# A post-layernorm transformer block on one core: the order of the last group's residuals and roots, and ScalarE's f16 high halves of the first two groups' rows eight steps earlier

## What is computed

```
x = layernorm(x + attention(x))     # 16 heads of 16, l2-normalised q and k, window of 128, alibi bias
x = layernorm(x + ffn(x))           # 256 -> 1024 -> 256
def ffn(x):
    h = gelu(x @ bw1.T + b1)        # bw = mean(|w|, axis=1) * sign(w)
    return h @ bw2.T + b2
```

## Time and profile before

| what | value |
|---|---|
| median of 3 runs | 369.43 us |
| the profiled execution | 370.22 us |
| its span, first to last instruction | 368.4 us |
| TensorE busy | 353.2 us (96%) |
| VectorE busy | 308.7 us (84%) |
| ScalarE busy | 307.3 us (83%) |
| GpSimd busy | 285.4 us (77%) |
| granted TensorE clock, mean | 0.997 |

### The profile page before, as it was taken

The page is one execution under the profiler, slowest core; times in us unless marked ns, Lnnn a source line. Parts: engine busy times, 40 slices in busy tenths (PEclk is TensorE's granted clock), DMA queues, the critical chain, the costliest instruction groups (busy, mean ns, idle before and its releaser), DMA issues. The chain is left out here.

```text
span 368.4 us, 13096 instructions
## 1 busy us (share of the span) xinstructions
PE 353.2 (96%) x4461; PEld 244.1 (66%) x4461; DVE 308.7 (84%) x771; ACT 307.3 (83%) x532; POOL 285.4 (77%) x440
## 2 busy tenths in 40 slices
PE   8789999999999999999999999999999999999992
PEld 5555676667766776776677677675666667667682
DVE  5977899898898898898899988879777887786775
ACT  3588888898898998898899999988888888887753
POOL 1188999889989999998999999757756856856433
PEclk9999999999999999999999999999999999999998
DMA  7678944744655646667767773303303513413113
GB/s 231 143 117 186 185 109 98 157 99 94 137 120 106 142 96 132 139 159 154 156 144 155 153 147 74 59 4 59 59 0 59 115 45 72 114 39 76 59 59 114
DMA packets 106884, 40.19 MB, mean 109 GB/s; under 512 B 92128, under 2 KB 105824, under 8 KB 106720
## 3 DMA queue, kind: packets, MB, share of 16 engines
q1 hardware_dynamic: 106848, 39.73, 49.6%
HBM read 12.72 MB, written 4.19 MB: 46 GB/s over the span
## 5 line engine op out<-in xcount | busy, mean ns | idle before, releaser
L1341 POOL TENSOR_SCALAR_AFFINE_SELECT prob<-prob 128x512 f32<-128x512 f32 x252 | 153.7, 646 | 11.1 <-ACT prob L700 11.1
L700 ACT ACTIVATE prob<-ps 128x1024 f32<-128x1024 f32 (+1 forms) x128 | 122.2, 1009 | 13.5 <-PE ps L390 13.4
L551 PE MATMUL ps<-yT,sgn 128*128 128x512 f16 x256 | 61.1, 379 | 0.0
L772 ACT ACTIVATE ps<-ps,bias,alpha 128x512 f32<-128x512 f32 x64 | 47.9, 750 | 15.6 <-PE ps L551 12.5
L421 PE MATMUL ps<-wqkv,xt 128*128 128x512 f32 x124 | 58.7, 596 | 1.2 <-DVE qkn L952 1.1
L411 PE MATMUL ps<-prob,vdiag 128*17 128x128 f32 x1024 | 51.3, 274 | 0.3
L411 PE MATMUL ps<-prob,vnext 128*17 128x128 f32 x992 | 49.9, 273 | 0.0
L1409 POOL TENSOR_TENSOR resid<-z,resid 128x256 f32 (+1 forms) x31 | 22.5, 726 | 29.9 <-DVE z L1173 29.9
L551 PEld LDWEIGHTS ps<-yT,sgn 128*128 128x128 f16 x256 | 25.0, 98 | 22.6
L390 PE MATMUL ps<-qkT 64*64 64x192 f16 (+2 forms) x1024 | 33.7, 248 | 2.8 <-DMA qkT<-parts 2.7
L454 PE MATMUL ps<-wo,oT 128*128 128x256 f32 x128 | 36.2, 405 | 0.1
(11 more groups left out here) (113 smaller groups left out, 690.2 us busy)
## 6 DMA issues: line engine op xcount, KB each, us to landing
xt<-in_xT SPq DMA_DIRECT2D x32, 128.0 KB, 2.1
resid<-in_x SPq DMA_DIRECT2D x32, 128.0 KB, 2.2
out_dram<-resid SPq DMA_DIRECT2D x7, 512.0 KB, 2.9
w<-in_w2T SPq DMA_DIRECT2D x1, 1024.0 KB, 7.7
w<-in_w1T SPq DMA_DIRECT2D x4, 256.0 KB, 3.3
w_nat<-in_w SPq DMA_DIRECT2D x4, 256.0 KB, 3.3
wqkv<-in_wqkvT SPq DMA_DIRECT2D x3, 256.0 KB, 3.9
qkT<-parts SPq DMA_TRANSPOSE x39, 4.3
```

The source lines that it names most:

```text
L551: mm = nc.tensor.matmul(ps[:, bank, :], sgn1[:, c, P * k:P * k + P], yT[:, par, a, c, :, :], start=(m == 0), stop=(m == 2 * DC - 1))
L700: nc.scalar.activation(to, scored, ACT.Exp, scale=QK_SCALE ** -2).then_inc(exp_done, 1)
L772: nc.scalar.activation(bank, bank, ACT.Gelu, bias=bias1[:, k:k + 1], scale=alpha1[:, k:k + 1]).then_inc(gelu_done, 1)
L1341: return nc.gpsimd.affine_select(out=at, in_=at, compare_op=ALU.is_ge, fill=0.0, base=-near, pattern=[[0, CH], [1 if near else -1, P]], ch ...
```

## The change

Two edits that don't touch each other.

The first: on ScalarE the loop now covers steps 4 to 15, and steps 16 to 23 are written out with one `high_y` at the end of each: group 0 in steps 16 to 19, group 1 in steps 20 to 23. They are gone from steps 24 to 29, and `high_pair` is gone.

The second, in the last group. VectorE takes both statistics of rows 0 and 1 ahead of `scale_out(g, 2)`, goes through the first half of the last block, and only then makes the shift for group 6; the shift for rows 0 and 1 comes after the last block's aggregate; rows 2 and 3 wait for roots 2 and 3 each by itself. GpSimd adds the residuals of rows 0 and 1 ahead of group 6's root, and the roots of group 7 are now of three columns (rows 0 to 2) and of one (row 3), in place of two and two.

```diff
-            with act.Fori(0, (NB - 12) // XS) as t:
+            with act.Fori(0, (NB - 20) // XS) as t:
                 for n in range(XS):
                     step(t * XS + 4 + n, n)
+            for n in range(2):
+                for b in range(XS):
+                    step(NB - 16 + n * XS + b, b, tail=lambda n=n, b=b: high_y(n, b, n))
...
-            step(NB - 8, 0, amid=lambda: signs1(0), tail=lambda: high_y(0, 0, 0))
+            step(NB - 8, 0, amid=lambda: signs1(0))
...
-            step(NB - 3, 1, next3=False, before_rows=lambda: signs2(1), tail=lambda: high_y(1, 1, 1))
+            step(NB - 3, 1, next3=False, before_rows=lambda: signs2(1))
...
             take_strips(NB - 2)
-            high_pair()
             gelu_of(0, 3, 0)
...
                 scale_out(g, 0, LAST_ZBANKS)
                 scale_out(g, 1, LAST_ZBANKS)
+                statistics(g, 0, 1)
+                statistics(g, 1, 1)
+                scale_out(g, 2, LAST_ZBANKS)
+                last_half(0)
                 end_shift(0, zmv[:, 0, :, 0], sixth)
-                statistics(g, 0, 1)
-                scale_out(g, 2, LAST_ZBANKS)
-                statistics(g, 1, 1)
-                last_half(0)
                 dve.wait_ge(zlast_sum, 1)
                 statistics(g, 2, 1, NB)
-                end_shift(1, zmv[:, 1, 0:2, 0], first)
                 last_half(1)
...
                 nc.vector.bn_aggr(zmv[:, 1, GB - 1, :], last_stats[:]).then_inc(zaggr, 1)
-                dve.wait_ge(end_rooted, 3)
+                end_shift(1, zmv[:, 1, 0:2, 0], first)
                 for b in (2, 3):
                     m = NB - GB + b
+                    dve.wait_ge(end_rooted, b)
...
                 pool.wait_ge(zaggr, summed)
+                count(pool, end_rooted, n)
...
+            add_residual(NG - 1, 0)
+            add_residual(NG - 1, 1)
             end_root_of(0, NB - GB, zmv[:, 0, :, 1], slice(0, GB))
-            for b in range(GB - 1):
-                add_residual(NG - 1, b)
-            end_root_of(1, NB - 2, zmv[:, 1, 0:2, 1], slice(GB, GB + 2))
-            end_root_of(2, NB, zmv[:, 1, 2:4, 1], slice(GB + 2, 2 * GB))
+            add_residual(NG - 1, 2)
+            end_root_of(1, NB - 1, zmv[:, 1, 0:3, 1], slice(GB, GB + 3))
+            end_root_of(2, NB, zmv[:, 1, 3:4, 1], slice(GB + 3, 2 * GB))
```

More of the change, by code:

```diff
@@ L741, in signs1, with high_y @@
                 nc.scalar.activation(sgn1[:, :, cols], w1_t[:, :, cols], ACT.Sign).then_inc(sgn_ready, 1)
+            def high_y(n, b, par):
+                act.wait_ge(y_done, n * GB + b + 1)
+                count(act, y_in[par], (n - par) * 8)
+                nc.scalar.activation(yparts[:, par, 0, :, b, :], resid4[:, n * GB + b, :, :], ACT.Copy).then_inc(yhi_done, 1)
             nc.scalar.preload_act_table_set("natural_log_exp_and_others")
@@ L796, in activate @@
                         high_y(n + 1, 3, 1 - par)
-            def high_pair():
-                high_y(1, 2, 1)
-                high_y(1, 3, 1)
             def last_signs():
@@ L806, in last_signs @@
                 signs2(3)
-            step(NB - 8, 0, amid=lambda: signs1(0), tail=lambda: high_y(0, 0, 0))
[L809 to L812, removed]
-            step(NB - 3, 1, next3=False, before_rows=lambda: signs2(1), tail=lambda: high_y(1, 1, 1))
+            step(NB - 8, 0, amid=lambda: signs1(0))
+            step(NB - 7, 1, amid=lambda: signs1(1))
+            step(NB - 6, 2, amid=lambda: signs1(2))
+            step(NB - 5, 3, amid=lambda: signs1(3))
+            step(NB - 4, 0, amid=lambda: signs2(0))
+            step(NB - 3, 1, next3=False, before_rows=lambda: signs2(1))
             step(NB - 2, 2, next2=False, next3=False, before_rows=last_signs)
```

## The result

The changed kernel takes 372.37 us (median of 6 runs, 371.75 to 372.69) against 369.55 us for the kernel before in the same comparison: a ratio of 1.0063, 95% interval [1.0033, 1.0093], or 2.3 us slower with 1.2 to 3.4 as bounds. A second comparison, of the same file, gave 1.0059 [1.0040, 1.0078]. The ratio is estimated apart from the medians and need not be their quotient, which is 1.0076 in the first comparison; so the loss is 2.3 us by the ratio and 2.8 by the medians. The forecast had the sign and both places. Its size, +1.2 us, was about half of what came, and the time lies above its range of 369.0 to 371.5.

The account below looks back on a forecast made before the run. With TensorE busy 353.2 of 368.4 us, only its mid-kernel gaps and the end after its last matmul could bring time. Terms 0 + 0 + 0.9 + 0.3 = +1.2 us gave a median of 370.6, range 369.0 to 371.5.

Parts of the forecast that it names:

- High halves in steps 16 to 23: Attention steps 16 to 23: ScalarE's idle time hides eight added operations; 0, kept between -0.1 and +0.4 us.
- High halves out of steps 24 to 29: Attention steps 24 to 29: ScalarE loses six operations, but GpSimd and VectorE set the pace; 0, ends -0.8 and +0.3 us.
- Rival (c): Steps 24 to 29 lose their gaps: -0.8, with +1.2 elsewhere 369.8 us; chance 0.10.
- high_pair: Before `outputs`: GpSimd's bias additions start early and hold four VectorE operations, so TensorE waits for `otok`; +0.9 us, bounds 0 to 1.4.
- 0.24 + 0.36 + 0.47 = about 1.1: Waits of VectorE's first and third small operations and of L961 beside GpSimd's additions, about 1.1 us together.
- The second slips in: VectorE's second small operation before `outputs` runs right behind the first without waiting for a GpSimd addition.
- The 0.36 for the third: Wait of VectorE's third small operation before `outputs`, taken as L870's: 0.53 - 0.16 us.
- The rule of the Trainium skill: VectorE's second SBUF port is shared with GpSimd and the two block each other, so the early additions cost time.
- The end: After 357.80 us: group 6's store goes out later and three stores queue at 345 GB/s; +0.3 us, from +0.1 to +0.35.
- rival (b): Last stores overlap better than one queue at 345 GB/s; end gains 0.5 to 0.7, time 368.8 to 369.0 us; chance 0.10.
- Rival (d): Steps 16 to 23 pay as VectorE comes late: +0.4 or more, 371.0 to 371.5 us; chance 0.60 together with the forecast.

Follow-up runs that it names:

- the gated kernel: High halves early, end as before, and GpSimd's eight bias additions made to wait until VectorE has made otok of block NB - 2: level with the kernel before.
- The parts: Two kernels, each with one edit against the kernel before: high halves alone, medians 1.5 us apart; end alone, medians 0.75 us apart.
- the third order: Kernel before with group 6's shift inside the last block's first half, ratio 1.0005; second form, rows 0 and 1's shift ahead of the second half, 0.9979.

## Why the prediction was right and wrong

**High halves in steps 16 to 23: right.** Forecast 0. ScalarE is busy 1.3 us more there, TensorE's eight steps take 57.31 in place of 57.44, and the gated kernel is level with before. The windows of exactly these steps, after and then before:

```profile
127.93:185.24 57.31, 57.31 (x912) 40.34 (x913) 51.86 (x128) 52.14 (x96) 52.99 (x81) 1.00 0.66 140
```

```profile
128.70:186.14 57.44, 57.44 (x913) 40.33 (x913) 51.61 (x128) 50.86 (x89) 53.08 (x81) 1.00 0.66 140
```

**High halves out of steps 24 to 29: nearly right.** Forecast 0, with ends of -0.8 and +0.3. Steps 24 to 31 took 54.70 to 55.16 us in the six traces with all high halves at their old places (54.9 in the mean) and 55.07 to 55.37 in the seven with some of them moved (55.15). So some 0.2 us may be lost there, with a scatter of the same size, and steps 16 to 23 give 0.1 of it back (57.3 in the six traces with the high halves there, 57.41 to 57.45 in the others). Rival (c), that the gaps of the earlier trace rows vanish, is refuted: the stretch got no shorter, and TensorE still waits for the same releaser (0.9 and 0.3 us in the two traces of the changed kernel). The 0.6 of the earlier trace rows is itself scatter: it is absent in the second trace of the kernel before.

**high_pair: the mechanism right, the size not.** Forecast 0.9, measured 1.46 to 1.52. The step that failed is "0.24 + 0.36 + 0.47 = about 1.1", with "The second slips in" in it. Measured are 0.41 + 0.49 + 0.49 + 0.30 = 1.69. I let an addition give way 0.47 us after its start, from one operation of 256 columns with one tensor input. For that kind it is right: less its own 0.41 us, L958 goes on 0.46 to 0.48 us after the start of the addition beside it in the four traces where it is held, and since it comes 0.17 behind that start, it loses 0.30 and not the 0.47 of the sum. Operations with two tensor inputs in SBUF, the core's working memory, go on later. L865 ends at 247.46; less its own 0.15 this is 247.31, and its addition, the second of the eight, started at 246.72, which is 0.59 before. In all traces this time is 0.58 to 0.61 us, for one column, four columns or 128. One such case stood in the trace of the kernel before, beside the residual that starts at 358.49: 358.55 + 0.68 - 0.14 = 359.09, 0.60 behind that start.

```profile
358.55 0.68 DVE L1245 SCALAR_TENSOR_TENSOR shift<-zmv,rnorm 128x4 f32<-128x4 f32 x1 [0.33 <-POOL rnorm L1434]
```

With 0.59 the first operation ends 0.59 + 0.15 = 0.74 us behind its addition's start, but the next addition starts at 0.69. So the second can't slip in, and VectorE gets one small operation in for each addition: each costs an addition's whole pitch less its own length and a step of 0.04 between the two, 0.69 - 0.16 - 0.04 = 0.49. The 0.36 for the third was L870's median beside cuts whose pitch is about 0.61; corrected to the additions' 0.69 it would have been 0.44. The other way, VectorE had 0.18 to spare and not 0.1, because the reciprocal follows the aggregate's start by 0.10 when nothing else holds it; with TensorE's 0.05 that is 0.23, and 1.69 - 0.23 = 1.46.

The rule of the Trainium skill that was weighed there ("Advanced Engine Details and Errata", "VectorE Performance Modes") is borne out in kind: the gated kernel is free of the cost, with all else the same. Its sentence names VectorE's 2-port instructions only, which the prediction left out; the runs show the hold also for two-input operations of one column, and none for the batch statistics.

**The end: right in kind, half the size.** Forecast +0.3, measured +0.61 to +0.64. The first half's scaling came at its hour (361.33 - 358.69 = 2.64 us, forecast 2.6). The addition behind it was held 0.48 us longer than its free length and not 0.27: 0.12 of the difference is the same mis-sized 0.47 (here 0.59), the rest that GpSimd's addition started 0.11 and not 0.20 ahead of it. So the store of group 6 went out at 6.32 and not at 6.1 us. The remaining 0.1 is the length of the block of data, 3.2 and not 3.04. That the last store stands in the queue of bytes was right, and rival (b), that the stores overlap better, is refuted: throughput is flat at about 340 GB/s, and taking 384 KB away gave back 0.4 us.

**The range.** Rival (d) had set its upper end with a cost of the attention steps that didn't come. The bounds of the two terms that did come, 1.4 and 0.35, lay below their values of 1.5 and 0.6; a hold bounded by the whole pitch of an addition for each operation (4 x 0.69 less their own 0.88, less the 0.15 to spare: 1.7) would have covered the first, not the second. With both sizes as the traces show them, 1.46 and 0.61, the sum is +2.1 and 371.5 us, the very end of the range. That the median of 372.37 lies outside is owed in part to what the traces don't show.

**What stays open.** The parts give 1.5 and 0.75 us by their medians, 2.2 in all, and 1.5 and 0.6 in the traces; the whole was 2.8 in the first comparison and 2.5 in the second. The two traces of the changed kernel have spans of 369.9 and 370.3, those of before 368.4 and 367.8, 2.0 apart in the mean. By the ratios nothing is missing between the parts and the whole (0.40% and 0.32% for the parts, 0.63% and 0.59% for the whole). The 0.3 to 0.6 us that the medians leave are within the intervals, as is the difference between the terms in the traces, 2.1, and the whole; no run tells whether they are more than scatter. That VectorE is held at the end of the kernel is read from the traces; no run took away that hold alone. Why steps 24 to 31 of one program scatter (54.79 and 55.09) wasn't followed up, nor what makes the 0.2 us there.

## What to carry to other kernels

A wait of an engine off the critical path can be what keeps it out of the way: before taking such a wait away, list what it will start, and which engine works beside it at that time. Where VectorE works with two inputs in SBUF beside a closed row of GpSimd instructions like the additions here, count one VectorE operation for each GpSimd instruction, however small the operation is. And at the end of a kernel count bytes back from the last store: a large store moved closer to it delays it even when the last rows themselves are ready earlier.

## What the runs showed of the hardware

- VectorE operations of one column, with two SBUF inputs, took 0.56 to 0.66 us beside GpSimd's 256-column additions (pitch 0.69) and 0.15 to 0.16 without them. A one-input operation of 256 columns took 0.71 for 0.41. Operations that read PSUM, TensorE's result memory (0.42), and the batch statistics on SBUF (0.41) kept their length beside the same additions.
- A held operation goes on a fixed time after the start of the addition beside it, whatever the operation's own length: 0.58 to 0.61 us with two SBUF inputs, 0.46 to 0.48 for the 256-column operation with one. The additions themselves are 0.73 us long.
- Little shows the other way: beside VectorE's shift and its held addition (0.78) in both forms of the third order, GpSimd's addition took 0.75 for 0.73 and the small operation behind it 0.24 for 0.20.
- A store's data begin 0.86 to 0.92 us after its issue when nothing is ahead of it. The three stores of the changed end, issued 1.09 and 0.42 us apart, ran as one block of about 340 GB/s.
